# A gated delta rule attention and feed-forward kernel: decay exponents from stored log sums, f16 pairs for the state products, the unit system on POOL, and new orders of the steps

## The reference

```python
qkv, z = x @ W_qkv.T, x @ W_z.T                  # q, k: 16 heads of 128; v, z: 32 heads of 128
beta  = sigmoid(x @ W_b.T)
decay = exp(-softplus(x @ W_a.T + dt_bias) * exp(A_log))      # one factor per token and value head
qkv_c = causal convolution with 4 taps; q, k = l2norm(q), l2norm(k)
def step(S, (q_t, k_t, v_t, b_t, d_t)):          # over the 256 tokens
    dv = b_t * (v_t - k_t . S)
    S  = S * d_t + outer(k_t, dv)
    return S, q_t . S
y = (rms_norm(out) * norm_w * silu(z)) @ W_out.T
h = silu(x2 @ w_gate) * (x2 @ w_up); keep the 2 largest of each 4; h @ w_down
```

## Time and profile before

| | us |
|---|---|
| median of 3 runs | 2107.87 (2105.32 to 2108.11) |
| the profiled execution | 2109.74 |
| its span in the profile | 2108.0 |
| PE busy | 2025.2 (96%) |
| weight loads (PEld) | 1672.9 (79%) |
| DVE busy | 1883.8 (89%) |
| ACT busy | 1663.7 (79%) |
| POOL busy | 1402.8 (67%) |

### The profile page before, as it was taken

The page is one execution under the profiler, slowest core; times in us unless marked ns, Lnnn a source line. Parts: engine busy times, 40 slices in busy tenths (PEclk is TensorE's granted clock), DMA queues, the critical chain, the costliest instruction groups (busy, mean ns, idle before and its releaser), DMA issues. The chain is left out here.

```text
span 2108.0 us, 61697 instructions
## 1 busy us (share of the span) xinstructions
PE 2025.2 (96%) x23974; PEld 1672.9 (79%) x23974; DVE 1883.8 (89%) x3120; ACT 1663.7 (79%) x3339; POOL 1402.8 (67%) x896
## 2 busy tenths in 40 slices
PE   4599999999999999999999999999999999998898
PEld 3278888888888888888888888888888888877787
DVE  5789999999999999999999999999999999985998
ACT  3488888888888888888888888888888888885332
POOL 3467667777667777766777766777776677763352
PEclk7799999999999999999999999999999999998999
DMA  2000000000000000000000000000000000002000
GB/s 93 20 2 22 2 22 2 22 2 22 2 22 2 4 20 2 22 2 22 2 22 2 22 2 22 2 3 21 2 22 2 22 2 22 2 22 91 6 26 21
DMA packets 12402, 34.06 MB, mean 16 GB/s; under 512 B 1100, under 2 KB 9420, under 8 KB 9684
## 3 DMA queue, kind: packets, MB, share of 16 engines
q1 hardware_dynamic: 12116, 30.11, 4.2%
HBM read 27.99 MB, written 2.11 MB: 14 GB/s over the span
## 5 line engine op out<-in xcount | busy, mean ns | idle before, releaser
L1595 DVE SCALAR_TENSOR_TENSOR cc<-bank,wc,cc 128x510 f32<-128x510 f32 (+2 forms) x768 | 533.8, 736 | 2.2 <-ACT cc L1143 2.0
L561 PE MATMUL bank<-h,w 128*128 128x512 f16 (+1 forms) x1920 | 421.0, 360 | 5.6 <-DVE cc L1595 3.8
L1671 DVE TENSOR_TENSOR yl<-bank,mask 128x512 f16<-128x512 f32 x384 | 263.6, 687 | 53.8 <-PE bank L561 53.8
L437 POOL TENSOR_TENSOR e_b<-ae,b_le 128x1024 f32<-128x1024 f32 x64 | 152.1, 2377 | 213.9 <-ACT ae L1208 213.9
L1224 ACT ACTIVATE inv<-bank 128x512 f16<-128x512 f32 x384 | 231.5, 603 | 74.3 <-PE bank L561 69.2
L561 PEld LDWEIGHTS bank<-h,w 128*128 128x128 f16 x1920 | 171.7, 98 | 144.0 <-DVE cc L1595 5.0
L402 POOL TENSOR_TENSOR g_le<-le,g_cols 128x1024 f16<-128x1024 f16 x128 | 241.0, 1904 | 20.5 <-DVE g_cols L1542 20.5
L1143 ACT ACTIVATE cc<-bank,wc 128x512 f32<-128x512 f32 x256 | 175.9, 687 | 93.5 <-PE bank L561 93.4
L1228 ACT ACTIVATE invT<-bank 128x512 f16<-128x512 f32 x384 | 232.7, 606 | 21.3 <-PE bank L561 21.3
L561 PEld LDWEIGHTS bank<-inv,a 128*128 128x128 f16 x3584 | 187.4, 98 | 58.9 <-ACT inv L1224 17.9
L561 PE MATMUL bank<-inv,a 128*128 128x64 f16 (+1 forms) x3584 | 218.8, 197 | 3.0 <-ACT inv L1224 3.0
(11 more groups left out here) (213 smaller groups left out, 5284.7 us busy)
## 6 DMA issues: line engine op xcount, KB each, us to landing
w_raw<-in_wh SPq DMA_DIRECT2D x16, 1032.0 KB, 4.8
v<-in_x SPq DMA_DIRECT2D x4, 512.0 KB, 3.9
out<-sol SPq DMA_DIRECT2D x16, 128.0 KB, 1.7
w_raw<-in_wgate SPq DMA_DIRECT2D x1, 1024.0 KB, 4.7
cc<-in_wup SPq DMA_DIRECT2D x1, 1024.0 KB, 4.8
pt<-gate_store SPq DMA_DIRECT2D x2, 512.0 KB, 4.5
ae<-in_wdown SPq DMA_DIRECT2D x1, 1024.0 KB, 6.6
sol<-gate_store SPq DMA_DIRECT2D x2, 512.0 KB, 5.9
```

The lines of the kernel that those rows point to most:

```text
L437: gp.tensor_tensor(e_b[:, :, 1:P + 1], e_raw, b_le[:], ALU.mult).then_inc(sig("eb"), 1)
L561: return mm(o_, l_, r_, start=start, stop=stop, skip_group_check=True)
L1595: V.scalar_tensor_tensor(dst, src, wc[:, par(s), i, 3 - j:4 - j], dst, ALU.mult, ALU.add).then_inc(sig(f"conv{i}"), 1)
L1671: V.tensor_tensor(lefts(yl[:, l], l), halves(bL[0], l), left(mask[:, l + 1, :], l).unsqueeze(1).broadcast_to([P, U, HP // n_, n_]), ALU.mu ...
```

## The change

1. Decay exponents. The running sums of the logs in a tile are made once in the setup: the logs are clamped to at least -80, cut into a coarse part on a grid and a fine rest, and eight f32 products of 128x128 sum them, already turned, in two PSUM banks. ACT and DVE cut each sum into a high and a low f16 half: four rows per tile and value head (RANK). SP stores them in DRAM (`rank_store`, after both halves) and loads for each step two times 32 rows of 128 f16 into partitions 64 to 71 of `moving` and `standing` (`load_rank`, two steps ahead, in SP's queue with the weight loads). The other 64 partitions hold constants that add a large negative number where s > t. So PE's `decay_product` is one f16 product of 128 columns over 72 rows for each unit, eight in a step. POOL's `decay_operand` and the tensors g_le, g_cols, le16 and gt16 go.
2. State products. ACT's `cross_kept` writes the f16 high half of kx (scaled by 1/16), the new DVE `cross_low` the rest; ACT's `scaled_high` writes the high half of `us`, POOL's `scaled_low` the rest; key_state and query_state are six f16 products of 128x256 each.
3. `unit_system` moves from DVE to POOL, as a select (affine_select) over 128x1024 that writes 1 on the diagonal and `at` elsewhere. It stands in the following iteration's POOL list.
4. The sixth level's mask (DVE) becomes a copy of the lower 64 partitions by ACT (`level_rows_last`).
5. Orders. In all four lists the six levels, residue and correction are now done in one iteration, for s1; the lists for s2 begin with refine. key_query moves ahead into the iteration of key_key. The products of the column sums (`decay_sums`), ACT's exponentials of them and DVE's column operations (`step_columns`, with the reciprocal and one operation more) move out of the setup into step 0, behind project 1 and conv1.

In the diff below the orders are written with several calls on a line and without their conditions; of ACT's list the first half stands, of DVE's the second.

```diff
@@ SP
+            sp.wait_ge(sig("beta_rank"), 2)
+            sp.dma_start(rank_store, rank_parts).then_inc(sig("gate_dma"), 16)
+            def load_rank(n):
+                need(sp, "e_ps", (n - 1) * 2)
+                src = rank_store[8 * hp_:8 * hp_ + 8, b_].rearrange("u k s -> k u s")
+                for side in range(2):
+                    dst = rank_rows(n % 2, side)[side:2 * RANK:2].rearrange("k (u s) -> k u s", s=P)
+                    sp.dma_start(dst, src).then_inc(sig(f"rank_in_{n % 2}"), 16)
@@ POOL
-                for part in range(2):
-                    gp.tensor_tensor(by_tiles(g_le[:, part]), over_tiles(le16[:]), g_cols[...], ALU.mult)
+            def scaled_low(s):
+                gp.tensor_tensor(us16[:, 1], us, us16[:, 0], ALU.subtract).then_inc(sig("usl"), 1)
+            def unit_system(s):
+                need(pool, "at", n + 1)
+                need(pool, "h_ps", (n - 1) * 2)
+                gp.affine_select(out=a1[:, ring(s)], in_=at, compare_op=ALU.not_equal, fill=1.0, base=0,
+                                 pattern=[[0, U], [1, P]], channel_multiplier=-1).then_inc(sig("a1"), 1)
             def body(s0, s1, s2, s3):
                 gate_output(s3)
+                unit_system(s1); first_inverse(s1); output_scale(s3); scaled_output(s3); scaled_low(s2)
+                queries_low(s0); low_half(s1); key_norm(s0); masked_beta(s0); decay_beta(s0)
@@ PE
             def decay_product(h, s):
-                for part in range(2):
-                    ins = m(bP[h][:], gt16[:], flat(g_le[:, part, us_]), start=(part == 0), stop=(part == 1))
+                for u in range(4 * h, 4 * h + 4):
+                    ins = m(bP[h][:, (u % 4) * P:(u % 4) * P + P], standing[0:K_, n % 2, u], moving[0:K_, n % 2, u])
             def key_state(s):
-                    ins = m(bS[1][:, g * C:g * C + C], kx[:, ring(s), g, 0], us[:, g * C:g * C + C])
+                need(pe, "ush", N(s) + 1); need(pe, "usl", N(s) + 1); need(pe, "kxl", N(s) + 1)
+                    ins = split_product(bk[:, g * C:g * C + C], [[kx16[:, ring(s), a, g, i] for a in range(2)]],
+                                        [[us16[:, a, g * C:g * C + C] for a in range(2)]])
             def body(s0, s1, s2, s3):
+                project(0, s0); turn_system(s1); key_cross(s1); refine(s2); level_rows(0, s1); turn_values(0, s1)
+                project(1, s0); level_left(0, s1); first_values(s2); project(2, s0); level_rows(1, s1)
+                turn_values(1, s1); level_right(0, s1); project(3, s0); level_right(1, s1); level_left(1, s1)
+                first_output(s2); level_rows(2, s1); turn_output(0, s3); turn_keys(s0); turn_queries(s0)
+                level_left(2, s1); key_state(s2); decay_product(0, s0); level_right(2, s1); level_rows(3, s1)
+                turn_output(1, s3); query_state(s2); second_values(s2); level_left(3, s1); project_output(0, s3)
+                level_right(3, s1); level_rows(4, s1); decay_product(1, s0); second_output(s2); z_rows(0, s1)
+                turn_normed(s0); level_right(4, s1); level_left(4, s1); project_output(1, s3); level_rows(5, s1)
+                key_key(s0); level_left(5, s1); key_query(s0); level_right(5, s1); residue(s1); z_rows(1, s1)
@@ ACT
             def inverse_right(l, s):
+                need(act, "left_ps", N(s) * NL + l + 1)
+            def level_rows_last(s):
+                A(yl[HP:P, YL, :, 0:HP], bL[0][HP:P, :], ACT.Copy, scale=-1.0).then_inc(sig("yt"), 1)
+            def scaled_high(s):
+                A(us16[:, 0], us, ACT.Copy).then_inc(sig("ush"), 1)
...
             def body(s0, s1, s2, s3):
+                last_tap(0, s0); cross_kept(s1); refined(s2); split_weights(s0); values_turned(0, s1)
+                last_tap(1, s0); inverse_left(0, s1); first_scaled(s2); first_kept(s2); last_tap(2, s0)
+                scaled_high(s2); inverse_right(0, s1); values_turned(1, s1); last_tap(3, s0); inverse_left(1, s1)
...
@@ DVE
+            def cross_low(s):
+                V.scalar_tensor_tensor(kx16[:, ring(s), 1], grid(bB[1]), 1.0 / KQ_SCALE, kx16[:, ring(s), 0],
+                                       ALU.mult, ALU.subtract).then_inc(sig("kxl"), 1)
-            def unit_system(s):
-                V.tensor_tensor(a1[:, ring(s)], at, ident16[...], ALU.add).then_inc(sig("a1"), 1)
             def body(s0, s1, s2, s3):
...
+                second_rest(s2); level_rows(3, s1); squared_norms(0, s0); squared_norms(1, s0); guarded_norms(s0)
+                output_low(1, s3); add_output(0, s3); split_weights(s0); second_output(s2); level_rows(4, s1)
+                output_sums(s2); keys_low(s0); add_output(1, s3); decayed_keys(s0); decayed_queries(s0)
+                z_gate(0, s1); correction(s1); z_gate(1, s1); first_inverse(s0)
```

More of the change, by code:

```diff
@@ L292, in load_weights @@
                 sp.dma_start(w_raw[:], wh[head]).then_inc(sig("w_dma"), 16)
-            for head in range(1, NK):
-                load_weights(head, head)
+            load_weights(1, 1)
+            for n in range(2, STEPS):
+                load_rank(n)
+                if n % NB == 0 and n // NB + 1 < NK:
+                    load_weights(n // NB + 1, n // NB + 1)
             sp.wait_ge(sig("w_lo"), NK * 4)
@@ L902, in body @@
                 if s1:
-                    need(pe, "vv", N(s1) * 2 + 1)
-                    turn_system(s1)
-                if s2:
-                    refine(s2)
+                    level_rows(1, s1)
+                    need(pe, "kx", N(s1) + 1)
+                    need(pe, "kxl", N(s1) + 1)
+                    turn_values(1, s1)
+                    level_right(0, s1)
                 if s0:
@@ L1357, in body @@
                 if s2:
-                    inverse_left(5, s2)
+                    refined(s2)
+                if s0:
+                    split_weights(s0)
                 if s1:
                     values_turned(0, s1)
-                    values_turned(1, s1)
-                    inverse_odds(s1)
-                    if not s0:
-                        gate_weights_high()
+                if s0:
+                    last_tap(1, s0)
+                    if N(s0) == 0:
+                        decay_factors()
+                if s1:
+                    inverse_left(0, s1)
                 if s2:
-                    inverse_right(5, s2)
+                    first_scaled(s2)
+                    first_kept(s2)
                 if s0:
@@ L1369, in body @@
                 if s2:
-                    refined(s2)
+                    scaled_high(s2)
+                if s1:
+                    inverse_right(0, s1)
+                    values_turned(1, s1)
+                    if not s0:
+                        gate_weights_high()
                 if s0:
                     last_tap(3, s0)
-                if s2:
-                    first_scaled(s2)
-                if s0:
-                    squares(0, s0)
-                if s2:
-                    first_kept(s2)
-                if s0:
-                    squares(1, s0)
-                if s1:
-                    inverse_left(0, s1)
-                    inverse_right(0, s1)
-                if s2:
-                    first_output(s2)
-                if s3:
-                    output_high(0, s3)
-                    output_high(1, s3)
-                if s2:
-                    query_part(s2)
-                    second_kept(s2)
                 if s1:
@@ new lines, in decay_columns @@
+                dve.wait_ge(sig("g_log"), 2)
+                V.tensor_scalar(log_part, glog, LOG_GRID, None, ALU.add).then_inc(sig("g_log"), 1)
+                dve.wait_ge(sig("g_log"), 3)
+                five = lambda ap: ap.rearrange("p (b t) (h v) -> p b t h v", t=TL, v=PV)
+                for b in range(NB):
+                    V.tensor_scalar(log_coarse[:, b], five(log_part)[:, b], -LOG_GRID, None,
+                                    ALU.add).then_inc(sig("g_log"), 1)
+                dve.wait_ge(sig("g_log"), 3 + NB)
```

489 lines of the change are left out of this document (282 added, 207 removed).

## The result

The changed kernel is slower: 2148.67 us median of 4 runs (2147.74 to 2152.97) against 2106.99 of the kernel before on the same chip, ratio 1.0204, 95% interval 1.0189 to 1.0219. The profiled execution took 2152.97, its span is 2151.2. The forecast was 2047.

A forecast was written before the change was run, and what follows sets the result against it. PE's issued work was taken to bound the kernel: step 28.55 − 0.63 − 0.42 = 27.5 us. 62 steps gave 2109.74 − 65.1 + 4.7 = 2049.3 for the profiled execution, 2047 as median; range 2027 to 2080.

The forecast's parts named there:

- A: Rival: ACT's operations cost their whole durations and ACT takes over; step 28.55, no gain, 2108 to 2113; chance 0.05.
- B: Rival: POOL's select takes 5.95 us, eight times 744 ns, late by 2.5 each step; about 2200; chance 0.07.
- the walk: One iteration of the new PE program, timed at trace prices: closes with about 0.3 us of waits, step 27.5.
- PE's prices: PE work per step: state products 1.94 to 1.31 us, gain 0.63; decay products 0.87 to 0.45, gain 0.42.
- with no gap left 27.2: Step time in us if PE's waits in the new order vanish; with them 27.5.
- The select: POOL's unit system as a select, eight times as wide as the 0.292 us one: 2.3 us at most.
- The rank loads … so nothing: SP's queue in later steps: two 8 KB loads have the better part of a step, so no cost.
- The setup's +4.7: Setup and step 0: column operations and low parts added, first convolution sooner; net +4.7 us, 0 to +9.
- The tail's 0: Last three iterations: same six levels one after another, only sooner; 0 us, −3 to +3.
- PE's issued work sets the step: Steady steps of 28.55 us: what PE gives up the step gains, until ACT, DVE or a chain binds.
- my 0.3 us of waits: PE's waits per step in the walk: 0.1 us at key_key, 0.2 at level 5.
- Rival C: Half the gain: semaphores or evictions 0.1 us later at four places, waits some 0.5, step 28.0, 2078; chance 0.18.

The follow-up runs named there:

- f12: f4 with PE's second output ahead of the second decay product, and ACT's key scaling and output squares before the second exponential: 2033.06 us, ratio 0.9654.
- f1: Changed kernel with DVE's split_weights, and the tap copies behind it, moved ahead of the two squared_norms: 2067.10 us, ratio 0.9806.
- f6: Kernel before with DVE's split_weights moved behind keys_low, beside POOL's decay_beta: 2174.38 us, ratio 1.0318.
- f2: Changed kernel with head 1's weight load issued ahead of the store of the log sums: 2151.81 us, ratio 1.0205.
- f3: Changed kernel with POOL's constants of moving and standing made later, after the logs and DVE's copies: 2140.08 us, ratio 1.0155.
- f4: Changed kernel with the edits of f1, f2 and f3 together: 2045.78 us, ratio 0.9706.
- f8: f4 with each decay product made twice: 2060.59 us, ratio 0.9775.
- f10: f4 with only high times high of the state products, 4 of 12 a step: 2046.89 us, ratio 0.9716.
- f5: Changed kernel with only the three tap-weight copies moved ahead of the squared_norms, the split left in place: 2108.24 us, ratio 1.000.

## Why the prediction was wrong

The sign was wrong, and neither rival for it (A, B) is what happened. The step that failed is the walk: it left DVE's weight split at its old 0.68 us, which measured 2.12, and each fourth step a tap copy at 0.16, which measured 2.31; beside it two things in the setup had been given no cost. By the steps:

- **PE's prices: right.** State products 1.31 forecast, 0.69 + 0.66 = 1.35 measured; decay products 0.45 forecast, 0.23 + 0.22 = 0.45. The Trainium skill's pair time of 81 ns (TensorE: Matmul & The Clock Gate, Back-to-back issue gap) is not what these rows show: 0.23 for four is 57 ns. The step "with no gap left 27.2": f12 has 27.37, with 0.09 and 0.18 us of gaps ahead of its second output projection and of the sixth level's left product, so 27.1.
- **The select: right.** 64 of 1.10 us, bound 2.3. Rival B's price was misread: the 744 ns are the mean of one select of 3.48 us and six of 0.29. The one stood from 37.81 to 41.29, through all three of DVE's subtractions (37.65 to 41.14), so the meeting cost no fixed factor on each select but the length of what one of them met.
- **The walk of one iteration: the step that failed.** It has second_output ending at 19.4 and "DVE's sum 20.3". In the trace after, PE ends it 1030.87 − 1011.59 = 19.3 us after the first projection, as walked, but DVE's sum starts at 20.5 (1032.08) and ends at 21.2, and the mask of level 4 behind it holds PE. The walk let DVE begin 0.2 us behind PE and never asked what stands on DVE ahead of the sum. It is `split_weights`, and I priced every DVE instruction at its duration from before. That duration held only because POOL did nothing at that moment (its `decay_beta` began at 1021.53, after the split of 1020.80 had ended). I had read from the earlier trace rows that a select of POOL stood beside two-input subtractions of DVE, and asked it of the new select alone, not of the instructions that moved. f1 (−82 us) and f6 (+66 us, on the kernel before) show that this is the cause.
- **"The rank loads … so nothing": wrong for head 1's weights.** The prediction looks at SP's queue in the later steps only. In the setup the weight load of head 1 was moved behind a store that waits for the log sums, 33 us later than before, and ACT's split waited 12.5 us. f2's step 3 came 9.2 us sooner.
- **The setup's +4.7: wrong by 17.6.** The sum has no term for POOL's constants. Of the 22.3 they cost 7.4 (f3) and the late weight load 9.2 (f2), each mended alone; mended together, in f4, they give 20.5, and the setup is +1.8 (145.13 for 143.31). So what the prediction did count stayed below its 4.7.
- **The tail's 0: wrong by 9, to the good.** From step 63's first projection to the last attention product (`w,goT`) it is 88.7 us (1997.34 − 1908.65), before 97.3 (1953.69 − 1856.41). I said that the last iterations keep the same six levels one after another. They do, but levels 4 and 5 no longer stand in an iteration of their own in front of the last refine. That this is the reason is read from the lists; no run sets it apart.
- **"PE's issued work sets the step": right for the kernel before, not for f4.** f4's 27.56 looks like my 27.5, but my 0.3 us of waits were laid at key_key (0.1) and level 5 (0.2); they are at the bank of goT (0.27), which the walk doesn't name, and at key_key (0.22), on one loop. Rival C's kind of cost was there, without its size.

By the Trainium skill (SBUF — State Buffer, Who interferes with whom) both halves of this follow: a DVE instruction with two SBUF inputs shuts out, or is shut out by, a GpSimd instruction that reads SBUF, but not one that only writes it, and copies and tensor_scalar forms with all operands in SBUF can do so in their two-port modes; whichever starts first keeps the other waiting for the whole instruction. The traces agree: 0.68 to 2.12 us for the split, 0.16 to 2.31 for a tap copy, 2.2 to 11.43 for eight copies. They agree on the exception too, a GpSimd instruction that only writes: seven products of DVE with two SBUF inputs (L1603) ran beside POOL's first fill (42.01 to 43.80) at 0.22 us each, as in the kernel before. I had the first half of the rule in the prediction, and used it on the one instruction that the change takes out.

## What to carry to other kernels

Before a list is reordered, put the new time tables of DVE and POOL side by side and mark every DVE instruction whose inputs all lie in SBUF: its duration of before may hold only at its place of before, even for a copy of four columns. Follow each DMA queue from the first instruction, not from the steady state: one load behind a new wait came 33 us late here and cost 9. And when all engines are 90% busy, find the loop that sets the step by adding and taking away work beside and on the path you suspect: f8 and f10 ruled out PE's work, and the loop that was left gave 12.7 us (f12).

## What the runs showed of the hardware

- An instruction that stands still behind POOL is shown as busy time of DVE: 122.8 for 41 us of splits. The profile names no wait; only the length, and POOL's row beside it, tell.
- POOL's fills and selects both stop DVE's f16 copies of 128x768. Of the eight, six took 1.24 us each, one beside each select of 1.1 to 1.2; two took 2.51 and 2.04, beside fills of 1.80 and 1.90. In f4, where POOL's come later, all eight take 2.23 together. DVE's f16 products with two SBUF inputs, 128x128, were not stopped by a fill.
- A wait of PE of 3.0 us can be followed by 3.4 us (0.56 in after) or 5.5 us (0.50 in f2) at or near 1.2 GHz, which makes the step 1.0 to 2.4 us longer for the same products; behind four of fifteen such waits in the kernel after the clock did not fall. Waits of 0.63 us in each step, 0.85 in each fourth, left it at 1.00 (f5).
- The select over 128x1024 takes 1.10 us on POOL, where its f32 products of that size take 1.90 (L464) to 2.57 (L474).
